# A selective scan with its inputs made for all batches first, and loads issued ahead of the layer norms

## The reference, cut to what matters

```
x = layernorm(x)                                  # first norm, kept as the residual
u = layernorm(x) * ln1_g + ln1_b                  # second norm, from the first one's result
xp, z = split(u @ W_in + b_in)                    # 512 channels each
xc = silu(causal_conv4(xp) + conv_b)
dtr, Bs, Cs = split(xc @ W_xp)                    # 16 + 16 + 16 columns
dt = softplus(dtr @ W_dt + b_dt)
h_t = exp(dt_t * A) * h_(t-1) + dt_t * xc_t * Bs_t    # 512 channels x 16 states
y_t = sum over states of h_t * Cs_t
x = x + ((y + xc * D_skip) * silu(z)) @ W_out + b_out
```

## Time and profile before

| | us |
|---|---|
| median of 3 runs (5630.48 to 5633.34) | 5632.72 |
| the profiled execution | 5629.68 |
| its span | 5627.8 |

### The profile page before, as it was taken

The page is one execution under the profiler, slowest core; times in us unless marked ns, Lnnn a source line. Parts: engine busy times, 40 slices in busy tenths (PEclk is TensorE's granted clock), DMA queues, the critical chain, the costliest instruction groups (busy, mean ns, idle before and its releaser), DMA issues. The chain is left out here.

```text
span 5627.8 us, 89667 instructions
## 1 busy us (share of the span) xinstructions
PE 4899.7 (87%) x37226; PEld 2802.5 (50%) x37226; DVE 2999.9 (53%) x5862; ACT 2219.3 (39%) x3543; POOL 1062.9 (19%) x660
## 2 busy tenths in 40 slices
PE   6879995999999999999899985666636999999897
PEld 3468884666666666666444442222213333333465
DVE  5757773555555555555100016778855666666360
ACT  5733432444444444444111114555512544445421
POOL 0145552111011011000000004446631000000021
PEclk9989997999999999999999997899867999999898
DMA  2221111000000000000200000000001000000122
GB/s 86 113 80 48 48 45 41 9 7 27 7 9 23 10 10 18 9 7 4 84 0 0 0 0 28 0 0 0 0 5 38 1 13 1 13 1 1 55 79 104
DMA packets 45384, 144.11 MB, mean 26 GB/s; under 512 B 6928, under 2 KB 18768, under 8 KB 38240
## 3 DMA queue, kind: packets, MB, share of 16 engines
q1 hardware_dynamic: 43472, 134.55, 6.7%
q0 software_dynamic: 1536, 4.20, 0.2%
HBM read 102.69 MB, written 36.04 MB: 25 GB/s over the span
## 5 line engine op out<-in xcount | busy, mean ns | idle before, releaser
L1471 DVE CUSTOM_DVE_ANT_0 ma_prob<-ma_ring,ma_mask 128x400 f32<-128x400 f32 (+1 forms) x1024 | 527.4, 572 | 260.0 <-PE ma_ring L1575 260.0
L1915 DVE TENSOR_REDUCE fa_part<-fa_ring 128x1 f32<-128x512 f32 x768 | 487.1, 681 | 221.9 <-PE fa_ring L2036 202.6
L1862 ACT ACTIVATE fa_prob<-fa_ring 128x512 f32<-128x512 f32 (+1 forms) x832 | 441.6, 598 | 407.6 <-PE fa_ring L2036 329.3
L2036 PE MATMUL fa_ring<-fa_K,fa_Q 32*128 32x512 f32 (+1 forms) x2048 | 532.2, 547 | 2.0
L1484 DVE COPY ma_PT<-ma_ring 128x512 f32<-128x512 f32 x512 | 342.0, 689 | 287.3 <-PE ma_ring L1585 286.9
L1585 PE MATMUL ma_ring<-ident,ma_prob 128*128 128x128 f32 (+1 forms) x3328 | 462.2, 280 | 6.7 <-ACT ma_prob L1430 6.7
L2056 PE MATMUL fa_ring<-fa_Qm,fa_K 32*128 32x512 f32 (+1 forms) x1664 | 458.8, 631 | 2.3 <-DVE fa_Qm L1932 2.3
L1599 PE MATMUL ma_pv<-ma_PT,ma_V 128*64 128x256 f32 (+1 forms) x3328 | 457.8, 393 | 0.0
L2245 PE MATMUL ffn_mid<-ffn_hid,ffn_h 128*128 128x512 f32 x1024 | 441.5, 593 | 9.7 <-DVE ffn_hid L2211 6.3
L1397 POOL TENSOR_SCALAR ma_diag<-ident,ma_rtotal 128x128 f32<-128x128 f32 x256 | 149.7, 602 | 1533.1 <-DVE ma_rtotal L1489 1533.1
L1585 PEld LDWEIGHTS ma_ring<-ident,ma_prob 128*128 128x128 f32 (+1 forms) x3328 | 357.1, 141 | 163.6 <-issue 105.1
(11 more groups left out here) (381 smaller groups left out, 7853.8 us busy)
## 6 DMA issues: line engine op xcount, KB each, us to landing
gd_rows<-gp_tile SPq DMA_DIRECT2D x16, 1024.0 KB, 4.2
gd_c_vg<-gd_rows SPq DMA_DIRECT2D x16, 1024.0 KB
moe_w<-in_moe_w SPq DMA_DIRECT2D x16, 1024.0 KB, 7.1
ma_w<-in_ma_w SPq DMA_DIRECT2D x32, 384.0 KB, 3.1
gd_rows<-gp_gate SPq DMA_DIRECT2D x16, 512.0 KB, 5.1
gd_c_qk<-gd_rows SPq DMA_DIRECT2D x16, 512.0 KB
ffn_h<-in_ffn_h SPq DMA_DIRECT2D x2, 4096.0 KB, 22.7
ma_ctxT<-in_ctxT SPq DMA_DIRECT2D x4, 1601.0 KB, 6.6
```

The source lines that it names most:

```text
L1471: nc.vector.tensor_tensor_reduce(prob[:, u % 2, t, h, k0:k0 + width], bank("S", u, t, n, h)[:, 0:width], mask[:, b % 2, half * 2 + t, k0:k ...
L1862: nc.scalar.activation(prob[0:n, (u * KT + kt) % PROBS, j, :], bank("scores", u, kt, j)[0:n, :], ACT.Exp, scale=SCALE).then_inc(p_ready, 1)
L1915: ins = nc.vector.tensor_reduce(part[:, u % 2, t, j, n:n + 1], src[:], AX, ALU.max)
L2036: last = nc.tensor.matmul(bank("chunk", u, i)[:, at * w:(at + 1) * w], Q[rows, b % 2, g, tile * P:(tile + 1) * P], K[rows, b % 2, g, k0:k0 ...
```

## The change

**Four layers.** The loads of constants move into a small block of their own ahead of the `layernorm` call, in masked attention, full attention, the ternary MLP, the scan and the waves. The block's engines other than SyncE have nothing to do in it. The first norm of the scan layer no longer turns and copies its result (`dst=None`), since the second norm overwrites it.

**Inputs of all batches in one block.** `scan_inputs` is straight code over 16 units `j` (batch and channel group). In each round TensorE projects x of unit `j+1` and z of unit `j`, while the previous batch gets its `dbc`, its time steps and the output projection of its skip term: `sz = xc * skip * silu(z)` is multiplied by `wout` and added to `xa` here, so it no longer goes through `y`. Silu(z) is written to DRAM (`kept`). After the 16 units the softplus of all batches is done in halves of 128x1024, with PSUM tiles `high` and `low` as work space, and GpSimd makes `dtx`.

**Sixty-four steps.** `scan_steps` is straight code over `g` = 0 to 63 on all engines, with `hC` in the memory of `xnT`. There is no meeting. The gating of batch `b-1` stands after step 0 of batch `b` on VectorE, its output projection and row additions in step 1 of batch `b`.

```diff
@@ layernorm
-            for g in range(GROUPS):
+            for g in range(GROUPS if dst is not None else 0):
@@ masked attention; the other layers likewise
+        with Scope(nc, "ma_load") as first:
+            block = first.block()
+
+            @block.sync
+            def _(sp):
+                sp.dma_start(w[:, 0], c.dram["ma_w"][0]).then_inc(w_loaded[0], 16)
...
+        layernorm(nc, c, "ma_ln", c.x, c.xnT)
@@ scan_inputs
+                for dst, src in ((win, "win"), (b_in, "bin"), (convw, "conv"), (conv_b, "conv_b"), (wxp, "wxp"), (wdt, "wdt"),
+                                 (b_dt, "bdt"), (neg_a, "A_log"), (skip, "skip"), (wout, "wout"), (pick, "pick")):
+                    sp.dma_start(dst[:], c.dram[f"scan_{src}"]).then_inc(loaded, 16)
+                sp.dma_start(b_out[:], c.dram["scan_bout"].partition_broadcast(P)).then_inc(loaded, 16)
+                sp.wait_ge(norms_loaded, 16)
+
+        layernorm(nc, c, "ss_ln0", c.x, None, keep=xa)
+        layernorm(nc, c, "ss_ln1", xa, c.xnT, gain=ln[:, 0, :], shift=ln[:, 1, :])
...
+            project_x(0)
+            for j in range(J + CC):
+                b, m = divmod(j, CC)
+                if j + 1 < J:
+                    project_x(j + 1)
+                if j < J:
+                    project_z(j)
+                if b >= 1 and m == 0:
+                    project_dbc(b - 1)
+                if b >= 1 and m == 1:
+                    project_step(b - 1, 0)
+                    project_step(b - 1, 1)
+                if b >= 1 and m == 2:
+                    project_step(b - 1, 2)
+                    project_step(b - 1, 3)
+                    project_out(b - 1, 0)
+                if b >= 1 and m == 3:
+                    project_out(b - 1, 1)
...
+            for k in range(2):
+                act.wait_ge(z_stored[k], B // 2 * SP_DONE)
+            act.wait_ge(sz_ready, B)
+            exponential(0)
+            exponential(1)
+            act.wait_ge(added, 2 * B)
+            act.wait_ge(parts_ready, B)
+            for i in range(4):
+                logarithm(i)
+            act.wait_ge(out_ready, 2 * B)
+            exponential(2)
+            exponential(3)
+            for i in range(4, 8):
+                logarithm(i)
...
+            one_more(0)
+            one_more(1)
+            for i in range(2 * B):
+                softplus(i)
+                if i + 2 < 2 * B:
+                    one_more(i + 2)
@@ scan_steps
+            def scans(g):
+                dve.wait_ge(dBx_ready, g + 1)
+                if g >= 1:
+                    dve.wait_ge(hC_ready, g)
+                    dve.wait_ge(hC0_ready, g)
                 for m in range(CC):
...
+            for g in range(G):
+                b, n = divmod(g, NS)
+                scans(g)
+                if b >= 1 and n == 1:
+                    add_out(b - 1)
+                against_C(g)
+                if b >= 1 and n == 0:
+                    gate(b - 1)
+            gate(B - 1)
+            add_out(B - 1)
...
+            for g in range(1, G):
+                b, n = divmod(g, NS)
+                spread_C(g)
+                if b >= 1 and n == 1:
+                    spread_B(g + 2)
+                    project_out(b - 1)
+                    pe.wait_ge(added, TB * b)
+                    add_up(g - 1)
+                else:
+                    add_up(g - 1)
+                    if g + 2 < G:
+                        spread_B(g + 2)
```

More of the change, by code:

```diff
@@ L1714, in full_attention, with _ @@
         ctxT = s.sb("ctxT", [P, DC, S2])
+        loaded = s.sem("loaded")
+        ctx_loaded = s.sem("ctx_loaded")
+        with Scope(nc, "fa_load") as first:
+            block = first.block()
+            @block.sync
+            def _(sp):
+                for dst, src in ((wq, "wq"), (wk, "wk"), (bqk, "bqk"), (wv, "wv"), (wo, "wo"), (sums, "sums"), (bv, "bv")):
+                    sp.dma_start(dst[:], c.dram[f"fa_{src}"]).then_inc(loaded, 16)
+                sp.dma_start(bo[:], c.dram["fa_bo"].partition_broadcast(P)).then_inc(loaded, 16)
+                sp.dma_start(ctxT[:], c.dram["ctxT"][0]).then_inc(ctx_loaded, 16)
+        layernorm(nc, c, "fa_ln", c.x, c.xnT)
+        bv_wide = s.sb("bv_wide", [P, FG, P])
         K = s.sb("K", [P, 2, FG, S2])
@@ new lines, in _ @@
+        @block.gpsimd
+        def _(pool):
+            pool.wait_ge(loaded, LOADS)
+            nc.gpsimd.tensor_tensor(xa[:], xa[:], b_out[:].unsqueeze(1).broadcast_to([P, NT, D]), ALU.add).then_inc(based, 1)
+            pool.wait_ge(sz_ready, B)
+            pool.wait_ge(dbc_ready, B)
+            for i in range(2 * B):
+                pool.wait_ge(dt_ready, i + 1)
+                x = pair(dtx[:, i // 2], i)
+                nc.gpsimd.tensor_tensor(x, pair(dt[:, i // 2], i), x, ALU.mult)
@@ L2352, in scan_channels, with scan_steps @@
+def scan_steps(nc, c, xa, kept, neg_a, wout, pick, dt, dtx, parts):
+    with Scope(nc, "scst") as s:
+        hC = c.xnT[:].rearrange("p a (m t) -> p a m t", m=CC)
+        zs = s.sb("zs", [P, CC, T])
         picked = s.sb("picked", [LOW + DBC, 2, 2, P], F32R)
@@ new lines, in decay @@
+            def decay(g, m):
+                q = CC * g + m
+                if q >= 2:
+                    act.wait_ge(scanned, q - 1)
+                nc.scalar.activation(dA[m % 2][:], dt[:, g // NS, m, :], ACT.Exp, scale=neg_a[:, m, g % NS:g % NS + 1]
+                                     ).then_inc(dA_ready, 1)
+            pick_rows(0)
+            pick_rows(1)
+            spread_row(0)
+            for g in range(G):
+                decay(g, 0)
+                decay(g, 1)
+                if g + 1 < G:
+                    spread_row(g + 1)
+                copy_C(g)
+                decay(g, 2)
+                decay(g, 3)
+                if g + 2 < G:
+                    pick_rows(g + 2)
@@ L2690, in waves @@
+            project_out(B - 1)
+def waves(nc, c, xa, ln):
     EDGE = 2
```

686 lines of the change are left out of this document (355 added, 331 removed).

## The result

The changed kernel takes 5574.55 us (median of 4 runs, 5567.64 to 5577.31), the kernel before in the same session 5633.03. The ratio is 0.9895, 95% interval 0.9878 to 0.9912. The forecast was 5559 with a range of 5532 to 5592: the sign and the range held, but 15.6 us of the forecast gain are missing. The profiled execution took 5576.27 (span 5574.4), 53.4 less than the profiled one of before, where the sum said 73.4. What follows compares these two, stage by stage.

The account below looks back on a forecast made before the run. VectorE bounds the scan's steps; inputs and tail are chains of waiting engines. Loads -36.1 and scan -37.3 give -73.4 from 5629.68, so 5556.3; the runs' median lies 3.04 higher: 5559 us, range 5532 to 5592.

Parts of the forecast that it names:

- Loads ahead of norms: Constant loads issued before the norm in five layers, the transfer running beside the norm: -36.1 us together.
- loads don't pay: Rival: SyncE's issue costs more or the norm slows beside the transfer; all of the -36 gone, 5595; chance 0.06.
- The input block: Scan inputs of all batches, TensorE the bound at 30.8 us a batch: 126.1 us, 173.5 with softplus.
- the last rival: Rival: TensorE at its lower clock in the input block, 112 us more at 1.2 GHz, 5671; chance 0.03.
- I am wrong if the input block passes 190: Sign against the forecast: the scan's input block, expected to last about 174 us, takes over 190.
- Softplus: End of the input block, TensorE idle, VectorE working through halves: 47.4 us with GpSimd's last product.
- VectorE and GpSimd did not block each other: Rival: the two engines block each other in the softplus, +18 us, 5577; chance 0.19 shared with gaps staying.
- The period: Time of one scan step: 6.58 us, taking the middle of VectorE's 0.57 us gap; all steps 421.0 us.
- the gaps go: Rival: step period 6.32 to 6.4 and cheaper input-block waits, -18 to -25 us, about 5538; chance 0.14.
- the gaps stay: Rival: VectorE's gaps in the scan steps remain, period 6.9, +20 us, 5579; chance 0.19 shared with softplus blocking.
- The borders: Three batch borders in the steps, with gating and output projection: 11.0 us each, 33.0 together.
- The end: After the scan's steps: tail and barrier 15.5 us as before, one more scope 0.7, so 16.2 us.

Follow-up runs that it names:

- loads_only: The kernel before, with only the load blocks ahead of the norm in masked attention, full attention and MLP; 5611.14 us, ratio 0.9962 to before.
- rows112: The changed kernel with time-step products over 112 rows instead of 16, zero rows added to the weights; 5554.47 us.
- dve_plain: The kernel before, with VectorE's two scan loops (batches and pairs of steps) written out; 5610.08 us, ratio 0.9954 to before.

## Why the prediction was right, and where it was off

- **Loads ahead of norms: right.** -38.2 against -36.1, each of the five terms within 2 us, and `loads_only` shows three of them without the rest. Up to each layer's first work the sum is met to a tenth, 36.1, which is partly luck: masked attention gives 8.8 and not 10.4, and the other places 1.6 more than forecast. The norms start 2.5 to 5.4 us later than before, under the 7 that would have told against the forecast. The rival "loads don't pay" is out.
- **The input block: the structure was right, TensorE's clock was the term mis-sized.** The forecast gave the clock 2.5 us, at the start. In `rows112`, where it holds from then on, the first 21.3 us to `dbc`, three batches of 30.8, 30.7 and 25.6 and the last 17.1 (the sum cuts the same work at other places) make 125.6 us against its 126.1, or 127.1 with the 1.0 for GpSimd, and the batch 30.73 against 30.8. Measured in the changed kernel: 8 to 25 us more, 24.7 in the profiled execution. The step that failed is the argument against the last rival: TensorE got 0.79 where it was busy 32 of 53 us, it would be busy nine tenths in the new block, and so the clock was given nothing behind the start. TensorE was busy nine tenths (139.2 of 150.5 us), and the granted clock was still 0.83. The case was weighed as all or nothing, at 112 us and a chance of 0.03; the truth is a part of it, behind two waits per batch. The kernel before had shown it: eight instructions of its time steps took 5.17, 5.05 and 4.92 us in three batches and 3.70 in the first, always behind 0.68 us of idle, in rows that the forecast did not use:

```profile
3606.81 5.17 PE L2629 MATMUL scan_y<-scan_low_rank,scan_wdt 16*128 16x512 f32 x8 [0.68 <-ACT scan_low_rank L2475]
```

  "I am wrong if the input block passes 190" was met in the execution compared here (195.0), and not in the two others of the same program (188.3 and 179.9).
- **Softplus: right.** 44.4 us against 47.4, VectorE's operations on a half at 1.22 us, GpSimd's at 2.35, and VectorE idle for 2.7 us behind the late third Exp, where 2.5 were taken. VectorE and GpSimd did not block each other there; that rival is out.
- **The period: too cautious.** 6.44 against 6.58, in 63 steps 9 us. The forecast kept half of the gap; `dve_plain` shows that nearly all of it came from VectorE's own loops (6.49 in most steps, where the work alone is 6.32). This is the rival "the gaps go", short of its 6.32 to 6.4 by 0.04 (and "the gaps stay" is out), and it hid 9 of the 20.5 us missed in the input block.
- **The borders: mechanism right, 37.0 against 33.** TensorE's projection runs partly at the lower level, 8.60, 9.14 and 9.42 us against the 7.17 of the sum, and the borders cost 11.9, 12.4 and 12.7 against 11.0.
- **The end:** 17.9 against 16.2. The last sum took 5.40 us (3.70 before) and the projection 8.62, against 7.17 at full clock: partly at its lower level, behind waits of 2.49 and 2.58 us. That is 3.0 us more up to the last addition; behind it 1.4 less passes than the sum had.
- **Not in the sum:** 3.9 us of the unchanged delta-net layer. Its end lay at 877.98 in the changed kernel and at 874.07 before. In the executions of all thirteen traces, with the same code up to there, that end lies between 873.9 and 880.2, so this is execution to execution.

The misses make up the 20 us between sum and profiled execution: +20.5 in the input block, -4.8 in steps and borders, +1.7 at the end, -2.7 for loads and start, +5.4 outside of the change.

Open is how the clock weighs idle time against products of few rows. The runs show five points (1.25 us with 16 rows: falls in 7 of 12 batches of four executions; 0.34 and less with 16 rows: falls in two of three batches, for 1.8 us; 1.26 with 112 rows: not in any of the waits of one execution; 1.66 once with 112 rows: not; 2.24 with 112 rows: falls in three of three, for 1.7 us), and that the first of them depends on the execution.

## What to carry to other kernels

Where TensorE is the bound, price each of its waits twice: once for itself, and once for what runs at half the clock behind it; look for the same instruction with two durations in the trace of before, which had the answer here. Products that use few rows are the place to look, and filling them with zero rows costs no time and gave back 20 us here. When a step or a loop is written out, look whether the idle time of the bounding engine behind its own results goes: here 0.45 of 0.57 us a step did; and where a bounding engine has to wait for another engine's result, let it do its next independent step first and order the other engine's queue to match (borders 37.0 to 17.5 us).

## What the runs showed that was not expected

- Eight products of 128x512 took 3.60 us or up to 6.59 in the same place of a program, with 1.25 us of idle and 16-row products ahead of them; with 112 rows and the same idle 3.60 at every place of the one execution traced.
- One program, three executions: 24.7, 18.0 and 8.3 us of TensorE's busy time lost to the lower level in one block of 320 products.
- A VectorE `tensor_scalar` over 128x64 with one SBUF operand took 7.25 us beside GpSimd's addition over 128x4096, and 0.20 with that addition cut to one row block. In the waves of the changed kernel the same happens to an operation of 128x6, beside an addition of GpSimd that started 0.02 us earlier and took 8.82 us; in the kernel before, VectorE's was first, and took 0.17:

```profile
4070.94 8.83 DVE L2993 TENSOR_SCALAR wave_gates<-wave_gates 128x6 f32<-128x6 f32 x1 [4.15 <-PEq L50]
```

  The prediction had quoted only half of the rule: the Trainium skill ("SBUF — State Buffer", "Who interferes with whom") exempts a single SBUF input only outside of VectorE's two-port modes, which it says `tensor_scalar` can enter. The trace agrees with the whole rule.
